# An accumulating DMA adds x1 to the residual rows, and the dense up products run in plain fp32

## The reference

```python
def attn(x, ...):                     # per batch
    h = layernorm(x, gamma, beta)
    h = spiral_conv(h, ...)           # a long convolution along the tokens, as a complex recurrence
    x1 = h + x
    h = layernorm(x1, gamma, beta)
    h = silu(h @ w1 + b1) @ w2 + b2   # w1: 128 x 512, w2: 512 x 128
    return h + x1

x = x + attn(plain_layernorm(x))      # so the sum is x + x1 + the dense part
x = x + moe(plain_layernorm(x))       # 8 experts, the best 2 of each token, 128 -> 256 -> 128
```

## Time and profile before

| | |
|---|---|
| median of the runs | 464.27 us |
| span of the profiled execution (first to last instruction) | 462.5 us |
| median less span: start and end outside it | 1.8 us |
| TensorE matmul, busy | 379.4 us, 82% |
| VectorE busy | 357.4 us, 77% |
| ScalarE busy | 321.8 us, 70% |
| GpSimd busy | 268.1 us, 58% |
| DMA, mean | 81 GB/s, 37.42 MB |
| mean granted TensorE clock | 0.934 of full speed |

### The profile page before, as it was taken

One profiled execution on the slowest core, in us unless ns is written; L12 is line 12 of the kernel. 1 busy time (PEld: TensorE's weight loads), 2 busy tenths in 40 slices (PEclk: granted clock), 3 DMA queues, 4 the chain that ended last, 5 costly groups with the idle time before them and its releaser, 6 DMA issues.

```text
span 462.5 us, 11382 instructions
## 1 busy us (share of the span) xinstructions
PE 379.4 (82%) x2812; PEld 339.3 (73%) x2812; DVE 357.4 (77%) x1329; ACT 321.8 (70%) x773; POOL 268.1 (58%) x331
## 2 busy tenths in 40 slices
PE   1274189989888889988897388999999999999980
PEld 1232168678676869686876388999999999999980
DVE  7999999978999999998176238777777777767770
ACT  4873387978887888867473536777777777777740
POOL 6980827452888888485627704676555555555551
PEclk9996569989999999999999569999999999999995
DMA  7649100000020202011203232444333333333200
GB/s 254 176 143 324 48 1 1 1 1 2 0 98 1 74 26 74 26 60 38 96 2 108 86 97 86 134 143 128 108 100 95 100 103 104 108 107 104 76 4 0
DMA packets 33283, 37.42 MB, mean 81 GB/s; under 512 B 5254, under 2 KB 29331, under 8 KB 33092
## 3 DMA queue, kind: packets, MB, share of 16 engines
q1 hardware_dynamic: 27236, 23.56, 18.0%
q0 software_dynamic: 5984, 13.13, 8.2%
HBM read 19.52 MB, written 18.92 MB: 83 GB/s over the span
## 4 chain that ended last, share of the span: by engine, by line
PE 56%; DVE 16%; ACT 9%; issue 5%; POOL 4%; POOLq 0%; DVEq 0%; ACTq 0%
PE up_p L999 12%; PE turn_p L999 6%; PE down_p L1018 6%; PE route_p L1018 6%; PE up_p L1018 5%; PE down_p L835 5%; PE turn_p L807 4%; DVE stats L1098 3%; ACT rows L655 3%; PE route_p L873 3%; ACT work L628 3%; PE down_p L1008 2%; DVE work L1162 2%; PE up_p L819 2%; DVE work L1160 1%
## 5 line engine op out<-in xcount | busy, mean ns | idle before, releaser
L590 POOL DMA_INDIRECT out<-result,out_id x91 | 89.2, 980 | 89.5 <-DVE result L1484 63.8
L556 POOL DMA_INDIRECT sorted_rows<-rows,pos x64 | 77.0, 1203 | 35.7 <-DVE pos L1217 18.4
L999 PE MATMUL up_p<-xt,work 128*128 128x128 f32 x488 | 66.5, 280 | 0.0
L781 ACT ACTIVATE work<-mw_c 128x256 f32 x182 | 65.5, 414 | 0.3 <-issue 0.2
L835 PEld LDWEIGHTS down_p<-w_sb,work 128*128 128x128 f32 x512 | 60.3, 192 | 4.9 <-issue 4.8
L835 PE MATMUL down_p<-w_sb,work 128*128 128x128 f32 x512 | 63.1, 277 | 0.0
L999 PEld LDWEIGHTS up_p<-xt,work 128*128 128x128 f32 x488 | 61.0, 196 | 0.2
L766 ACT ACTIVATE hid_t<-up_p 128x512 f32<-128x512 f32 x61 | 36.4, 597 | 30.3 <-PE up_p L999 29.7
L807 PE MATMUL turn_p<-ident,work 128*128 128x128 f32 x192 | 28.6, 298 | 28.4 <-ACT work L641 10.9
L615 ACT ACTIVATE work<-up_p,b_all 128x512 f32<-128x512 f32 x64 | 41.5, 680 | 14.3 <-PE up_p L821 14.2
L807 PEld LDWEIGHTS turn_p<-ident,work 128*128 128x128 f32 x192 | 24.0, 154 | 34.4 <-ACT work L641 11.6
(11 more groups left out here) (244 smaller groups left out, 896.5 us busy)
## 6 DMA issues: line engine op xcount, KB each, us to landing
tin<-sorted_rows SPq DMA_DIRECT2D x91, 136.0 KB, 2.1
resid<-in_x SPq DMA_DIRECT2D x8, 512.0 KB, 3.8
sorted_rows<-zeros SPq DMA_DIRECT2D x29, 136.0 KB, 2.3
out<-result,out_id POOLq DMA_INDIRECT x91, 2.2
work<-in_mw SPq DMA_DIRECT2D x1, 1024.0 KB, 6.2
sorted_rows<-rows,pos POOLq DMA_INDIRECT x64, 2.5
work<-in_w SPq DMA_DIRECT2D x1, 256.0 KB
w_sb<-in_w SPq DMA_DIRECT2D x1, 256.0 KB
```

Source lines behind the costliest of these rows:

```text
L556: g.indirect_dma_start(sorted_dram, bass.IndirectOffsetOnAxis(pos[b % 2][:, j:j + 1], 0), rows[b % ROWBUFS][:, j, :], None).then_inc(s_sor ...
L590: g.indirect_dma_start(out_rows, bass.IndirectOffsetOnAxis(out_id[k][:, :], 0), result[k][:, :], None, bounds_check=TOKENS - 1, oob_is_err ...
L781: last = s_.activation(ring[s % RING][:, k * EF:(k + 1) * EF], mw1_c[:, bass.ds(at[k], EF)], ACT.Copy)
L999: last = t.matmul(mid_p[s % DEEP][:, c * TILE:(c + 1) * TILE], ring[s % RING][:, c * 128:(c + 1) * 128], xt[s % DEEP][:, :], start=True, s ...
```

## The change

x1 no longer goes into `down_p`. GpSimd issues, per batch, one DMA that adds x1 to the batch's rows of `resid` in SBUF (512 KB, 128 partitions x 4 KB), behind the scales of x1 and x2 and ahead of x's; the x2 sum waits for its semaphore. The four chunks' up products are one fp32 product per half, of `w1_g` and of `h_t`, the unsplit copy of the turned h2. The low half, `w1_hi`, `w1_lo` and the wait `s_lo` go; TensorE waits for ScalarE's copy instead. The diff, cut to its core:

```diff
@@ gpsimd
+            def add_x1(b):
+
+                pool.wait_ge(s_x1, b + 1)
+                pool.wait_ge(s_hn, b + 1)
+                pool.wait_ge(s_xn, b + 1)
+                g.dma_start(batch_of(resid, b), x1[b % 2], accum_op=ALU.add).then_inc(s_res[b], 16)
...
                 if live(b0):
                     x2_scales(b0)
+                if live(b1):
+                    add_x1(b1)
                 if live(b3):
                     x0_scales(b3)
...
             x1_scales(0)
             x0_scales(2)
+            add_x1(0)
@@ scalar
-                s_.activation(h_hi[:, :], turn_p[:, :], ACT.Copy).then_inc(s_hi, 1)
+                s_.activation(h_t[:, :], turn_p[:, :], ACT.Copy).then_inc(s_hi, 1)
...
-            s_.activation(b2_hi, b2_rows, ACT.Copy).then_inc(s_aw, 1)
-            s_.activation(w1_g, w1_sb, ACT.Copy, scale=par[:, GAMMA:GAMMA + 1]).then_inc(s_aw, 1)
+            s_.activation(b2_hi[:, :], b2_rows, ACT.Copy).then_inc(s_aw, 1)
+            s_.activation(w1_g, w1_sb, ACT.Copy, scale=par[:, GAMMA:GAMMA + 1])
             a.wait_ge(s_aw, 1)
-            s_.activation(b2_first, b2_hi.bitcast(f32), ACT.Copy, scale=ident[0:2, 0:1])
-            a.wait_ge(s_aw, 2)
-            s_.activation(w1_hi[:, :], w1_g, ACT.Copy).then_inc(s_whi, 1)
+            s_.activation(b2_first, b2_hi[:, :].bitcast(f32), ACT.Copy, scale=ident[0:2, 0:1]).then_inc(s_whi, 1)
@@ tensor
                 if c == 0:
-                    pe.wait_ge(s_lo, b + 1)
+                    pe.wait_ge(s_hi, b + 1)
...
-                    t.matmul(dst, w1_hi[:, k], half(h_lo, h), start=True, stop=False)
-                    t.matmul(dst, w1_hi[:, k], half(h_hi, h), start=False, stop=False)
-                    t.matmul(dst, w1_lo[:, k], half(h_hi, h), start=False, stop=True).then_inc(s_up, 1)
+                    t.matmul(dst, w1_g[:, k], half(h_t, h), start=True, stop=True).then_inc(s_up, 1)
...
-                    for h in range(2):
-                        t.matmul(half(down_p, h), ident[:, :], x1[b % 2][:, h * TPB // 2:(h + 1) * TPB // 2, :],
-                                 start=False, stop=False, skip_group_check=True)
...
-                after(pe, s_lo, b)
+                after(pe, s_hi, b)
@@ vector
                 v.wait_ge(s_dn, (b + 1) * FC)
+                v.wait_ge(s_res[b], 16)
...
-            def scans(b, rotated, between=None):
+            def scans(b, rotated):
...
-                if between:
-                    between()
...
-            def low(b):
-                v.wait_ge(s_hi, b + 1)
-                d.tensor_tensor(h_lo[:, :], turn_p[:, :], h_hi[:, :].bitcast(f32), ALU.subtract).then_inc(s_lo, 1)
...
-                if live(b1):
-                    low(b1)
...
-                                       op0=ALU.mult, op1=ALU.add)
-                d.tensor_tensor(w1_lo[:, :], w1_g, w1_hi[:, :].bitcast(f32), ALU.subtract).then_inc(s_wsplit, 1)
+                                       op0=ALU.mult, op1=ALU.add).then_inc(s_wsplit, 1)
...
-            scans(1, rotated, lambda: low(0))
+            scans(1, rotated)
```

More of the change, by code:

```diff
@@ L87, in block_moe_kernel @@
         par = sb("par", [128, COLS])
-        w1_hi = sb("w1_hi", [128, FF], f32r)
-        w1_lo = sb("w1_lo", [128, FF], f32r)
         w2_sb = sb("w2_sb", [128, FC, D])
@@ L95, in block_moe_kernel @@
         ident = sb("ident", [128, 128])
-        h_hi = sb("h_hi", [128, LENGTH], f32r)
-        h_lo = sb("h_lo", [128, LENGTH], f32r)
+        h_t = sb("h_t", [128, LENGTH])
+        b2_hi = sb("b2_hi", [2, HALF], f32r)
         mw1_c = sb("mw1_c", [128, EXPERTS * EF])
@@ L122, in block_moe_kernel @@
         b2_rows, b2_lo = work[0:2, 12, 0:HALF], work[0:2, 12, HALF:LENGTH]
-        b2_hi = h_hi[0:2, 0:HALF]
         b2_first = work[0:2, 13, 0:HALF]
@@ L295, in block_moe_kernel @@
         s_t3 = sem("h2_turned")
-        s_hi = sem("h_hi_ready")
-        s_lo = sem("h_lo_ready")
+        s_hi = sem("h_turned_copied")
         s_up = sem("up_done")
@@ L300, in block_moe_kernel @@
         s_dn = sem("down_done")
+        s_res = [sem(f"x1_in_residual{b}") for b in range(BATCHES)]
         s_x2 = sem("x2_ready")
@@ L1315, in weights @@
                 v.wait_ge(s_whi, 1)
-                link(d.tensor_tensor(b2_lo, b2_rows, b2_hi.bitcast(f32), ALU.subtract))
+                link(d.tensor_tensor(b2_lo, b2_rows, b2_hi[:, :].bitcast(f32), ALU.subtract))
                 d.scalar_tensor_tensor(out=b2_hi_lo[:, :], in0=b2_lo, scalar=ident[0:2, 1:2], in1=b2_first,
-                                       op0=ALU.mult, op1=ALU.add)
-                d.tensor_tensor(w1_lo[:, :], w1_g, w1_hi[:, :].bitcast(f32), ALU.subtract).then_inc(s_wsplit, 1)
+                                       op0=ALU.mult, op1=ALU.add).then_inc(s_wsplit, 1)
                 v.wait_ge(s_b1raw, 1)
```

## The result

The changed kernel takes **460.52 us** (median of 4 runs, 459.66 to 462.13) against 464.37 for the kernel before beside it; ratio 0.9915, interval 0.9892 to 0.9938. Two more measurements of the same kernel gave 0.9934 and 0.9937. The forecast of 461.8 us and its range held, and so did "faster". The profiled span is 457.9 us against 462.5: 4.6 us less. The forecast had 2.5, and its parts were not all right. The profiled execution of the changed kernel took 459.66 us, the least of its four, against 464.27 for that of the kernel before, so the spans lie further apart than the medians (3.9 us).

The account below looks back on a forecast made before the run. Bound: VectorE in iterations 2 and 3, a loop through all engines in 4 and 5. Start -2.15, iterations 2 to 4 -1.1, iterations 5, 6 and end +0.8: -2.5 us, from 464.27 to 461.8 us; range 458.8 to 466.5.

Parts of the forecast that it names:

- The up products' price: TensorE: a plain fp32 up product takes two records, 0.86 us at full clock, against 0.69 us split; +1.4 us per batch.
- rival D: More gained: scatters not late (-0.7), full clock sooner (-0.8), no half-clock stretch in iteration 1 (-1.7); 458.6 us; chance 0.13.
- the half-clock stretch of iteration 1: TensorE at half clock some 4 us over x2's turn and up chunk 3; expected to stay, fp32 products costing 0.2 to 0.4 more.
- The start: Up to batch 3's x1 sum: 2.15 us earlier, without VectorE's low half and its wait for ScalarE's copy.
- Iterations 2 to 4: Dense loop: 24.4, 25.1 and 24.5 us, together 74.0 against 75.2, so 1.1 us gained.
- The 0.9 us of lateness of GpSimd in iteration 3: GpSimd, with moments 1.14 us earlier, is 0.9 us late with the scales; iteration 3 takes 25.1 us.
- The DMA: GpSimd's issue before x0's scales takes 1.3 us, hidden by 4.4 us of cover less 0.9; no x2 sum waits for its landing.
- A: Rival: the accumulate's issue on GpSimd is the bound, between x2's scales and the scatters; 472.1 us at 7.7 us issue; chance 0.13.
- B: Rival: the issue takes about 4 to 5 us on GpSimd; only the start's gain remains; 463.3 us; chance 0.17.
- C: Rival: the accumulate lands so slowly that an x2 sum or the scatters behind it are late; 466 us; chance 0.05.
- The identity products stand nowhere in that loop: Iterations 4 and 5: the loop through all engines holds the last up products, not the identity products (1.8 to 1.9 us per batch).
- Iterations 5, 6 and the end: Loop-bound iterations 5 and 6 lose 0.3 us each, the stretch behind batch 6's x2 sum 0.2; together +0.8 us.

Follow-up runs that it names:

- c1: The kernel before, with 16 extra identity transposes on TensorE ahead of its first wait for x2; 463.16 us, ratio 0.9968.
- p5: p2 with the bias products repeated three more times in the place of the identity products; 466.77 us, ratio 1.0062 to the kernel before.
- p6: p2 with the identity products kept as work for nothing, so only the DMA differs from the kernel before; 468.78 us, ratio 1.0097.
- p1: The kernel before with the fp32 up products alone; identity products stay, no accumulating DMA; 463.64 us, ratio 0.9994.
- p7: p6 with the DMA issued behind x0's scales, still before the scatters; 464.43 us, ratio 0.9999 to the kernel before.
- p4: The changed kernel with each batch's accumulating DMA cut into four of two tiles each; 473.94 us, ratio 1.018 to the kernel before.
- p2: The kernel before with the accumulating DMA instead of the identity products; up products stay split; 466.64 us, ratio 1.0056.
- p3: The changed kernel with the DMA issued behind the scatters, last of GpSimd's work in an iteration; 463.09 us, ratio 0.9971 to the kernel before.
- m1: The changed kernel with the DMA issued behind x0's scales and before the scatters; 461.13 us, ratio 0.9937 to the kernel before.

## Why the prediction held, and where it did not

**The up products' price** was right: 0.86 us each at the full clock (four records in 1.72 us).

**As a whole**, the time lies between the forecast (461.8) and rival D (458.6, chance 0.13). All three terms of D came in the first profile: the scatters were not late, the full clock came sooner, and the half-clock stretch of iteration 1 did not come. The sum stayed near the forecast mainly because iterations 5 on gave back 0.65 us more than I had. That the number held owes something to luck.

**The start** was right in kind: the x1 sum of batch 1 came 1.8 us earlier (1.7 forecast), that of batch 2 a further 1.0 (2.8 in all, 2.3 forecast). The half microsecond goes with a term of rival D that I had kept out: the full clock comes sooner. In the third measurement, where it came 1.3 us later than in the first, the x1 sum of batch 2 was only 1.8 us earlier. That this lateness is the cause is not shown.

**The half-clock stretch of iteration 1** is where the forecast failed most. I had kept it ("TensorE's wait before it gets longer, not shorter") and put the x1 sum of batch 3 at 2.15 us earlier; it came 4.5 earlier. The wait did get longer, 2.45 instead of 2.07 us, and the stretch did not come, in any of the three profiles of the changed kernel. c1 measures its worth at 1.6 us in the kernel before. The inference from the length of a wait to the clock was wrong: p5 and p6 have 2.06 us there and kept the clock, the kernel before, p1 and p7 have 2.06 or 2.07 and lost it, p4 has 2.45 and lost it, p2 has 3.12 and lost it. What decides it is open. So about 1.6 of the 4.6 us of span came by the clock and not by work taken out; the remaining 3.0 stand beside the forecast of 2.5. Whether the edit brings these 1.6 is open too. Of the 27 executions of the kernel before timed beside p1 to p3, fourteen had a mean granted clock of 0.933 or 0.934, like the profiled one, and a median of 464.56 us; seven had 0.937 or 0.938 and 463.24. Perhaps those ran without the stretch; no profile shows it.

**Iterations 2 to 4** were forecast at 24.4, 25.1 and 24.5 and took 24.49, 24.52 and 24.40. The terms that bound them were right (VectorE's 25.5 less its low half; the loop). The 0.9 us of lateness of GpSimd in iteration 3 did not come: the fifth scatter took 0.96 us instead of 1.86, since VectorE's operations stood elsewhere.

**The DMA** was sized rightly at 1.3 us (0.91 to 1.12 us of issue and 0.3 to the next) and so was its landing (4.6 us; I had 3.8), so rivals A, B and C did not hold. But the sentence that x0's scales come later "and ScalarE uses them only at the end of the iteration" asked only who waits for them, and not what they run beside. Moved by some 1.1 us they grew by 4 us in p6, and made the scatters and then x1's scales late. I had counted the issue as free in iterations 4 and 5; in the changed kernel its chain costs 0.3 to 0.5 us in iteration 5 (m1), in p6, with the clock, 3.3. I had weighed, from the Trainium skill (SBUF — State Buffer, "Who interferes with whom"), that a VectorE instruction with two SBUF inputs and a GpSimd instruction that reads SBUF exclude one another, and asked it of the issue alone. The operations of 0.22 and 0.21 us that took 2.30 and 1.49 us in p6 agree with that rule, for each ended within 0.05 us of a scan or a product of VectorE; it had to be asked of everything that the issue pushes. Not all rows agree: in p6 a power on 16 values (170.64 us, 2.93) had begun before a scan (171.21 us, 2.34) and ran on beside it, and neither took longer than elsewhere (2.90 and 2.34). So the two instructions do not exclude one another for their whole length there.

**"The identity products stand nowhere in that loop"** was true of the kernel before and misleading for the change. p1 shows that the fp32 products put them on the path at once. Neither half of the change gained by itself: p1 0.9994, p2 1.0056, together 0.9915 to 0.9937. That the halves need each other is shown in part only: half of what p1 lacks in the profiles is its half clock in iteration 1, and p2 loses by the place of its issue and by the clock. p7 (0.9999) keeps the identity products as work for nothing, so it says that the DMA costs nothing in a better place, not what their removal gives. Whether p2 with its issue placed as in p7 would gain was not tried.

**Iterations 5, 6 and the end** were forecast to give back 0.8 us and gave back 1.45: 0.8 instead of 0.3 in iteration 5, which is GpSimd's chain, and 0.3, 0.3 and 0.05 behind it. The expert part then took 0.2 us longer.

## What to carry to other kernels

When an instruction is put into a queue, ask of each instruction that it pushes what the other engines do at its new time, not only who waits for it: here the same issue cost 4.4 us or nothing, depending on whether it stood before or behind five small operations. Before a part of a change is costed as off the path, redo the path with the change's other part in place. And where a profile has a half-clock stretch, an edit can win or lose by it: it cost 1.6 us in iteration 1 of the kernel before and under 0.1 us in iteration 5 of the second profile of the changed kernel, where TensorE had a wait to spend. Test it with a filler, as c1 did with full-width products, before crediting the edit.

## What the runs showed of the hardware

- The granted clock does not follow the length of the wait alone. Ahead of the same instruction, waits of 2.06 us were followed by half clock in three kernels and by full clock in two; waits of 2.45 to 2.48 us by full clock in six profiles and by half clock in one; one of 3.12 us (p2) by half clock.
- Products of two rows did not keep it up: right behind 2.10 us of them, with TensorE busy throughout, the clock fell to 0.50 (p5, iteration 5), and it did so within 1.2 us behind them in six of the eight batches. With full-width products in the same place (p6) it fell in none of these places.
- A GpSimd operation on 8 values per partition that takes 0.2 us alone took 2.3 us in p6 under a scan, and 3.0 and 3.5 in p4, where the DMA issues overlap its start. A power on 16 values took 4.8 instead of 2.9 when it began under a scan (p4), and 2.9 when a scan began under it (p6).
- An accumulating DMA of 512 KB took 0.99 us to issue, whole, and landed in 4.6 us; in four pieces, of the same bytes together, the issues took 3.70 us and each piece landed in 3.4. What GpSimd pays for here is the number of issues.
